# A fused attention and feed-forward layer on one core: fewer and earlier first loads, batch 1 normalised ahead, two moves in the last block

## The chip, the core and the metric

The kernel runs on one core of one Trainium2 chip. TensorE (PE) does the matmuls and the transposes, VectorE (DVE), ScalarE (ACT) and GpSimd (POOL) work beside it, and SyncE (SP) issues the DMAs. Each engine runs its own list of instructions strictly in order and meets the others by semaphores. The metric is the device time of one execution in microseconds; the number given for a kernel is the median of its runs.

## The reference

All data are float32. For x of shape (4, 512, 256) the layer is

```
x = x + layernorm(attn(layernorm(x)))
x = x + layernorm(ffn(layernorm(x)))
```

`attn` adds two things and multiplies the sum by Wo. The first is attention of 2 heads of 128 in windows of 128 tokens, each looking at its own and the previous 128 keys. The second is a memory that learns while it reads: for each of 4 batches and 4 heads of 64 it keeps three 64x64 states W0, W1, W2 and goes through the sequence in 4 chunks of 128 tokens:

```
q, k = l2norm(silu(x @ Wq)), l2norm(silu(x @ Wk));  v = silu(x @ Wv)
out  = (silu(q @ W0.T) * (q @ W2.T)) @ W1.T          # read with the chunk's states
dW*  = gradients of the same net for k, v and rates l0, l1, l2, plus momentum M* * mean(m)
dW*  = newtonschulz5(dW*)                            # 5 rounds: A = X X', B = bA + cAA, X = aX + BX
W*   = renorm(W* + dW*)                              # rows keep their first norm
```

The rates come from a softplus of x @ Wlr, m from a sigmoid of x @ Wm + bm; the read result is normalised, scaled by o_norm_g and by silu(x @ Ws + bs). `ffn` is a gelu layer 256 -> 1024 -> 256 with biases.

## The kernel before

The work is cut into 4 chunks of 128 tokens, each for all 4 batches. Every engine walks through the same written list `ORDER` of steps and does its own part of each step, if it has one. A step is written KIND.chunk.rest: `QK.0.1` is the product of chunk 0, batch 1, with the q and k weights. The list alone sets the order on PE, DVE, ACT and POOL. SP has its own code (lines 461 to 505), which doesn't follow the list. `bank_plan` goes through the list once and gives each step that writes PSUM the banks that come free first, so a step that leaves the list changes the banks of those behind it.

The steps that the change and the prediction speak of:

- `LN1.0.b` (line 1067): DVE takes mean and variance of the rows of batch b (line 1070, 1072), POOL makes the inverse root in two instructions, an addition of the epsilon (line 1424) and a power (line 1419). `LNX.0.b` (line 1087): DVE subtracts and multiplies. `XT.0.b` (line 536): PE transposes the rows, ACT copies them to `xnT` (line 816).
- `QK.0.b` (line 559) and `VV.0.b` (line 568): PE multiplies with the q/k weights (512 columns) and with the v weights and the 20 small ones (276 columns). Each float32 matmul instruction stands as two passes in the trace, so a QK step of two instructions is x4. ACT copies q and k to `raw` (line 816), DVE copies v to `v_rows` (line 1127) and adds the small biases (line 1135).
- `SI` (lines 873, 874): silu on ACT. `NQ`: square on ACT (line 886), sum on DVE (line 1141), root on POOL (line 1419). `NR`: reciprocal on DVE (line 1147), product on POOL (line 1419, `silu<-silu,rq`). `TR.0.0` to `TR.0.9` (line 591): transposes of q, k, v for the attention (0 to 3, from `raw`) and for the memory (4 to 9).
- `LN1.1`, `LNX.1`: the same normalisation for chunk 1, all batches at once; its rows come by `rows_in(1)`.
- `WI.0` (lines 1350 to 1361 on DVE, 1022 on ACT): DVE spreads the loaded states over the batches into `W`, ACT squares them. `WX.0.g` (line 723): PE transposes the states, ACT copies them to `WT02` and `W1T`.
- `SP.0`: rates on ACT and DVE. `S.0.b` (line 732): scores, masked on DVE (line 1298). `WN.0`: DVE sums the squares of the states (line 1365), which `FW.0.0` on ACT waits for (line 937). `DW.0` (line 662): the gradients, fed by `ELB` on DVE.
- `F2.3.b` (line 793): the last product of batch b; DVE adds the bias, takes statistics (lines 1378 to 1382), POOL makes the inverse root (lines 1424, 1419). `F2N.3.b` (lines 1387, 1056): DVE subtracts the mean, then multiplies by the inverse root and adds `x1`; SP stores (line 491).

Before the list PE runs 9 matmuls on a tile of ones (line 808), whose result nobody reads.

The signal that a DMA has landed is counted by a semaphore of its own per group: `ld_qkv`, `ld_small`, `ld_misc`, `ld_w`; `first_x[b]` for the rows of chunk 0.

Of the kernel before, what the change touches and what calls it, by code (L numbers as in the profile page):

```python
# [128 lines left out]
def steps(text):  # L129
# [17 lines left out]
    TR.1.3 NB.0.1.1 NB.0.1.2 NT.0.0 MS.1 NT.0.1 NT.0.2 NT.0.3 NX.0.1.0 NX.0.1.1 NX.0.1.2 TX.0.2.0 NQ.1.0 TX.0.2.1
    TX.0.2.2 NQ.1.1 SI.1.3 F1.0.0 NA.0.2.0 NA.0.2.1 NA.0.2.2 F1.0.1 F1.0.2 LN1.2 NB.0.2.0 NB.0.2.1 NB.0.2.2 NQ.1.2
    NR.1.0 NR.1.1 F1.0.3 F1.0.4 LNX.2 NX.0.2.0 NX.0.2.1 NX.0.2.2 NQ.1.3 TX.0.3.0 TX.0.3.1 TX.0.3.2 F1.0.5 NA.0.3.0
    NA.0.3.1 WR.0 NA.0.3.2 XT.2 F1.0.6 NB.0.3.0 NB.0.3.1 NB.0.3.2 MM.1 NR.1.2 NR.1.3 NX.0.3.0 NX.0.3.1 NX.0.3.2  # L150
    TX.0.4.0 KL.1.0 TX.0.4.1 TX.0.4.2 F1.0.7 NA.0.4.0 NA.0.4.1 NA.0.4.2 KL.1.1 TR.1.4 TR.1.5 F2.0.0 SP.1 NB.0.4.0
# [5 lines left out]
    WON.1.1 NA.1.0.0 NA.1.0.1 NA.1.0.2 SI.2.0 SI.2.1 CT.1.2 CT.1.3 L2.1.0 VV.2.2 VV.2.3 NB.1.0.0 NB.1.0.1 NB.1.0.2
    WO.1.2 WO.1.3 NQ.2.0 LN1.3 MS.2 L2N.1.0 NQ.2.1 NX.1.0.0 NX.1.0.1 NX.1.0.2 TX.1.1.0 WON.1.2 WON.1.3 TX.1.1.1
    TX.1.1.2 QK.2.3 NA.1.1.0 NA.1.1.1 NA.1.1.2 NB.1.1.0 NB.1.1.1 SI.2.2 NT.1.0 L2.1.1 L2.1.2 L2.1.3 L2N.1.1 TR.2.0
    TR.2.1 TR.2.2 TR.2.3 MM.2 NB.1.1.2 NX.1.1.0 NX.1.1.1 SM.2 NX.1.1.2 NR.2.0 L2N.1.2 NT.1.1 NT.1.2 L2N.1.3 TX.1.2.0  # L160
    TX.1.2.1 NR.2.1 LNX.3 TX.1.2.2 NT.1.3 NA.1.2.0 F2N.0.0 NA.1.2.1 SI.2.3 NQ.2.2 NQ.2.3 NA.1.2.2 NR.2.2 NR.2.3 KL.2.0
# [1417 lines left out]
```

## Time and profile before

| | |
|---|---|
| median of 3 runs | 382.04 us (381.73 to 382.21) |
| span of the profiled execution, first to last instruction | 380.1 us (380.141) |
| median less span | 1.9 us |
| PE busy | 371.0 us, 98% of the span |
| DVE, ACT, POOL busy | 257.6, 213.3, 193.9 us |
| bytes read from HBM, written | 7.73 MB, 2.10 MB |

The profiled execution has no time of its own beside its span. The span counts from the first to the last instruction; what lies around it is taken as the 1.9 us by which the median is above it. Times below are in microseconds from the start of the span. A busy PE isn't PE at its peak: its matmuls are pipelined and their ends modelled, so that the starts of two matmuls tell more than the length of one.

### The profile page before, as it was taken

To read this page: it belongs to the slowest core of one execution; us is meant where nothing else is said; L and a number is where in the kernel's file an instruction comes from. 1 tells how busy PE (TensorE), PEld (TensorE's weight loads), DVE (VectorE), ACT (ScalarE), POOL (GpSimd) and SP (SyncE) were. 2 spreads that over 40 slices of the span, in tenths; PEclk is the share of its full clock that TensorE was granted. 3 is DMA by queue.
4 is the path that set the end of the run, shared out by engine and by line. 5 is a ranking of instruction groups with operands and counts; after the bars stand their busy time and mean duration, and the time that the engine had idled before them with its cause. 6 is when DMAs were issued, how large, how long until landed. Compare 5 with 4: busy or idle time off the path is not lost.

```text
span 380.1 us, 15979 instructions
## 1 busy us (share of the span) xinstructions
PE 371.0 (98%) x6760; PEld 295.4 (78%) x6760; DVE 257.6 (68%) x682; ACT 213.3 (56%) x432; POOL 193.9 (51%) x290
## 2 busy tenths in 40 slices
PE   8999999999999999999999999999999999999994
PEld 5588688856788877878578888688887757988883
DVE  4678998674278699898546746987875492767124
ACT  1799855766512766649743346665358575614500
POOL 4399865356239457475963434364333340557212
PEclk9999999999999999999999999999999999999999
DMA  5562200001000000000000200000000110000101
GB/s 156 121 238 60 83 1 6 3 3 46 16 3 2 3 3 2 3 4 5 16 19 17 71 16 3 2 2 17 20 3 4 40 36 2 0 3 0 57 0 55
DMA packets 12677, 10.84 MB, mean 29 GB/s; under 512 B 4544, under 2 KB 12096, under 8 KB 12608
## 3 DMA queue, kind: packets, MB, share of 16 engines
q1 hardware_dynamic: 12608, 9.83, 8.9%
q8 instruction: 54, 0.88, 1.0%
q14 instruction: 15, 0.12, 0.1%
HBM read 7.73 MB, written 2.10 MB: 26 GB/s over the span
## 4 chain that ended last, share of the span: by engine, by line
PE 86%; DVE 4%; SPq 3%; issue 2%; POOL 2%; ACT 1%; DMA 1%; POOLq 0%; DVEq 0%; ACTq 0%
PE pair L782 15%; PE pair L793 15%; PE pair L713 6%; PE pair L701 6%; PE pair L691 6%; PE pair L559 6%; PE pair L682 5%; PE pair L591 4%; PE pair L763 3%; PE pair L732 3%; PE pair L568 3%; PE pair L748 3%; PE pair L662 2%; PE pair L739 2%; PE pair L629 1%
## 5 line engine op out<-in xcount | busy, mean ns | idle before, releaser
L782 PE MATMUL pair<-xn2T,p1T 128*128 128x512 f32 (+1 forms) x160 | 59.1, 512 | 0.0
L793 PE MATMUL pair<-p2T,h 128*128 128x256 f32 x256 | 57.0, 379 | 0.0
L793 PEld LDWEIGHTS pair<-p2T,h 128*128 128x128 f32 x256 | 48.0, 190 | 6.4 <-issue 0.2
L1424 POOL TENSOR_SCALAR var<-mv 128x1 f32<-128x1 f32 (+1 forms) x55 | 13.1, 239 | 67.1 <-DVE mv L1382 37.4
L1034 ACT ACTIVATE h<-pair,b 128x512 f32<-128x512 f32 (+1 forms) x40 | 23.9, 602 | 36.0 <-PE pair L782 35.9
L782 PEld LDWEIGHTS pair<-xn2T,p1T 128*128 128x128 f32 x160 | 28.7, 190 | 17.1 <-issue 14.8
L1419 POOL TENSOR_TENSOR nq<-ssq,half 128x8 f32<-128x8 f32 (+1 forms) x16 | 24.2, 1513 | 27.5 <-DVE ssq L1141 27.5
L1056 DVE SCALAR_TENSOR_TENSOR A<-pair,eye 128x512 f32<-128x512 f32 x45 | 28.7, 683 | 13.2 <-PE pair L691 13.1
L1419 POOL TENSOR_TENSOR rstd<-var,neg_half 128x1 f32<-128x1 f32 (+1 forms) x55 | 33.5, 609 | 4.6
L1056 DVE SCALAR_TENSOR_TENSOR B<-pair,eye 128x512 f32<-128x512 f32 x45 | 28.9, 684 | 10.2 <-PE pair L701 10.0
L559 PE MATMUL pair<-wqkv,xnT 128*128 128x512 f32 x64 | 31.5, 627 | 0.6 <-ACT xnT L816 0.6
L701 PEld LDWEIGHTS pair<-A 64*64 64x64 f32 x1440 | 23.7, 134 | 7.5 <-issue 4.6
L987 ACT ACTIVATE masked<-masked,nmax 128x256 f32<-128x256 f32 (+1 forms) x32 | 15.1, 474 | 25.5 <-DVE nmax L1298 25.5
L823 ACT ACT_TABLE_LOAD x22 | 28.2, 1283 | 1.1 <-PEq L1569 0.7
L691 PEld LDWEIGHTS pair<-XT 64*64 64x64 f32 x1440 | 23.3, 134 | 6.3 <-issue 5.7
L816 ACT ACTIVATE XT<-pair 128x512 f32<-128x512 f32 x45 | 24.6, 600 | 6.4 <-PE pair L682 6.4
L713 PEld LDWEIGHTS pair<-X,B 64*64 64x64 f32 x1440 | 23.6, 134 | 5.0 <-issue 2.7
L959 ACT ACTIVATE X<-pair 128x512 f32<-128x512 f32 x36 | 19.8, 598 | 13.2 <-PE pair L713 13.1
L701 PE MATMUL pair<-A 64*64 64x64 f32 x1440 | 26.5, 221 | 0.3 <-issue 0.3
L713 PE MATMUL pair<-X,B 64*64 64x64 f32 x1440 | 26.1, 221 | 0.1
L691 PE MATMUL pair<-XT 64*64 64x64 f32 x1440 | 25.8, 221 | 0.3 <-ACT XT L816 0.2
L682 PE MATMUL pair<-ident,X 128*128 128x128 f32 x180 | 24.1, 276 | 0.5 <-ACT X L959 0.3
(165 smaller groups left out, 775.4 us busy)
## 6 DMA issues: line engine op xcount, KB each, us to landing
x_in<-in_L_attn_x_dram SPq DMA_DIRECT2D x16, 128.0 KB, 2.5
x<-in_L_attn_x_dram SPq DMA_DIRECT2D x16, 128.0 KB, 2.1
out_dram<-rows_a SPq DMA_DIRECT2D x16, 128.0 KB, 1.7
p1T<-in_L_ffn_proj_dram SPq DMA_DIRECT2D x1, 1024.0 KB, 4.7
p2T<-in_L_ffn_proj_dram SPq DMA_DIRECT2D x1, 1024.0 KB, 7.4
wqkv<-in_L_attn_Wqkv_dram SPq DMA_DIRECT2D x1, 768.0 KB, 4.8
wo<-in_L_attn_Wo_dram SPq DMA_DIRECT2D x1, 256.0 KB, 7.7
X<-in_L_attn_w_dram SPq DMA_DIRECT2D x6, 32.0 KB, 2.2
```

What stands on the lines that cost most here:

```text
L559: mm_ = pe.matmul(ps, xnT[:, k, b * P:(b + 1) * P], wqkv[:, k, 0:512], start=(k == 0), stop=(k == KC - 1))
L682: mm_ = pe.transpose(ps[:, b * P:(b + 1) * P], X[:, g, 2 * b:2 * b + 2, :], ident[:, :])
L691: mm_ = pe.matmul(BANK[bank[0] + row][64 * col:64 * col + 64, n * HD:(n + 1) * HD], xt, xt, start=True, stop=True)
L701: mm_ = pe.matmul(BANK[bank[0] + row][64 * col:64 * col + 64, n * HD:(n + 1) * HD], a, a, start=True, stop=True)
L713: mm_ = pe.matmul(BANK[bank[0] + row][64 * col:64 * col + 64, n * HD:(n + 1) * HD], B[64 * row:64 * row + 64, g, 4 * (row ^ (slot & 1)) + ...
L782: mm_ = pe.matmul(ps[:, at], p1T[:, k, n * P:(n + 1) * P], xn2T[:, k, at], start=(k == 0), stop=(k == KC - 1))
L793: mm_ = pe.matmul(ps[:, 0:DIM], h[:, n, b * P:(b + 1) * P], p2T[:, n, :], start=(n == 0), stop=(n == HC - 1))
L816: return act.activation(dst, src, ACT.Copy)
L823: act.preload_act_table_set(name)
L1034: act.activation(h[:, n, at], BANK[bank[0]][:, at], ACT.Gelu, bias=b1[:, n:n + 1]).then_inc(S["h"].sem, 1)
L1056: return dve.scalar_tensor_tensor(out=out_, in0=in0, scalar=scalar, in1=in1, op0=op0, op1=op1)
L1419: return pool.tensor_tensor(out_, in0, in1, op)
```

## The change

It has four parts.

1. The loads at the start. The weights of q, k, v and the small ones stand in one array `Wall`, whose first 512 columns (q and k) are loaded before the rows of batches 1 to 3 and the other 276 behind them; seven loads of constants are one (`packed`, 356 columns per partition, the rows already repeated over the partitions). The three states come already spread over the batches and also transposed (`states`, 128 partitions x 3072), into `W`, `WT02` and `W1T`. So DVE's copies of `WI.0`, the steps `WX.0.*` and one memset are gone. The arrays are laid out outside the kernel (`laid_out`). SP now follows the list as well, with the steps `XI.c` (rows of chunk c for the normalisation) and `XA.c` (rows for the residual).
2. `LNX.0.1` stands before `LN1.0.3` and `CO.0`. Behind the transposes of batch 0 (`XT.0.0`) PE runs 3 matmuls of 64 columns on the tile of ones, whose result nobody reads.
3. At the end `F2N.3.2` stands before `F2.3.3`.
4. For the last block (chunk 3, batch 3) the epsilon is added on DVE, and POOL only takes the power.

```diff
-    LN1.0.0 XT.0.0 LNX.0.0 LN1.0.1 LN1.0.2 CO.0 LN1.0.3 LNX.0.1 QK.0.0 XT.0.1 LNX.0.2 LNX.0.3 VV.0.0 VV.0.1 SI.0.0
+    LN1.0.0 XT.0.0 LNX.0.0 LN1.0.1 LN1.0.2 LNX.0.1 LN1.0.3 CO.0 XA.0 QK.0.0 XT.0.1 LNX.0.2 LNX.0.3 VV.0.0 VV.0.1
...
-    F1.3.6.1 F1.3.7.1 F2.3.0 F2.3.1 F2N.3.0 F2.3.2 F2N.3.1 F2.3.3 F2N.3.2 F2N.3.3
+    F1.3.1.1 F1.3.2.1 F1.3.3.1 F1.3.4.1 F1.3.5.1 F1.3.6.1 F1.3.7.1 F2.3.0 F2.3.1 F2N.3.0 F2.3.2 F2N.3.1 F2N.3.2
+    F2.3.3 F2N.3.3
...
             sp.dma_start(x_in[:, 0, :], x[0, 0:CHUNK, :]).then_inc(first_x[0], 16)
-            sp.dma_start(wqkv[:, :, 0:3 * DIM], Wqkv.rearrange("(k p) n -> p k n", p=P)).then_inc(ld_qkv, 16)
+            sp.dma_start(wqkv[:, :, 0:512], Wall[:, 0:512].rearrange("(k p) n -> p k n", p=P)).then_inc(ld_qkv, 16)
             for b in range(1, BATCH):
                 sp.dma_start(x_in[:, b, :], x[b, 0:CHUNK, :]).then_inc(first_x[b], 16)
...
-            sp.wait_ge(ld_qkv, 16)
-            for n, w in enumerate((w1, w2, w0)):
...
-            rows_in(1)
+            sp.dma_start(wqkv[:, :, 512:], Wall[:, 512:].rearrange("(k p) n -> p k n", p=P)).then_inc(ld_v, 16)
+            sp.dma_start(packed_in[:, :], packed).then_inc(ld_misc, 16)
+            sp.dma_start(W[:, :, :, :], states[:, 0:1536].rearrange("p (g s d) -> p g s d", s=8, d=HD)).then_inc(ld_w, 16)
+            sp.dma_start(WT02[:, :, :, :, :], states[:, 1536:2560].rearrange("p (b j k d) -> p b j k d", j=2, k=2, d=HD)).then_inc(ld_wT, 16)
+            sp.dma_start(W1T[:, :, :, :], states[:, 2560:3072].rearrange("p (b j d) -> p b j d", j=2, d=HD)).then_inc(ld_wT, 16)
+            XI(1)
...
                     mm_.then_inc(S["first_xT"].sem, 1)
+                    if b == 0:
+                        for n in range(3):
+                            pe.matmul(BANK[7][:, 0:64], ones[:, :], ones[:, 0:64], start=True, stop=True)
                     return
...
                 dve.bn_aggr(mv4[:, b, :], st4[:, b, :]).then_inc(S["f2_mv"].sem, 1)
+                if ends(c, b):
+                    dve.wait_ge(*S["f2_mv"](c, b + 1))
+                    dve.tensor_scalar(var4[:, b:b + 1], mv4[:, b, 1:2], LN_EPS, None, ALU.add).then_inc(S["f2_var"].sem, 1)
...
             def F2(c, b):
+                if ends(c, b):
+                    wait_apart(pool, S["f2_var"](c, b + 1))
+                    tt(rstd4[:, b:b + 1], var4[:, b:b + 1], neg_half[:, 0:1], ALU.pow).then_inc(S["f2_rstd"].sem, 1)
+                    return
                 rsqrt(c, b + 1, mv4, var4, rstd4, "f2_mv", "f2_var", "f2_rstd", slice(b, b + 1))
```

How the lists of instructions change, at three places. First SP at the program's start, before and then changed (`Wlr`, `Wm`, `Ws`, `bm` and so on are the small inputs; `in_L_attn_w_dram` a state; `first_xn` rises when batch b is normalised):

```order
L462 DMA wqkv<-in_L_attn_Wqkv_dram 128x2x768
L464 DMA x_in<-in_L_attn_x_dram 128x256 x3
L465 DMA wqkv<-in_L_attn_Wlr_dram 128x2x12
L466 DMA wqkv<-in_L_attn_Wm_dram 128x2x4
L467 DMA wqkv<-in_L_attn_Ws_dram 128x2x4
L468 DMA small_bias<-in_L_attn_bm_dram 128x4
...
L479 DMA X<-in_L_attn_w_dram 64x2x64 [waits ld_qkv]
L479 DMA X<-in_L_attn_w_dram 64x2x64 x5
L459 DMA x_in<-in_L_attn_x_dram 128x256 [waits s_first_xn]
L459 DMA x_in<-in_L_attn_x_dram 128x256 x3
```

```order
L473 DMA wqkv<-in_Wall_dram 128x2x512
L475 DMA x_in<-in_L_attn_x_dram 128x256 x3
L476 DMA wqkv<-in_Wall_dram 128x2x276
L477 DMA packed_in<-in_packed_dram 128x356
L478 DMA W<-in_states_dram 128x1536
L479 DMA WT<-in_states_dram 128x1024
L480 DMA W1T<-in_states_dram 128x512
L464 DMA x_in<-in_L_attn_x_dram 128x256 [waits s_first_xn]
L464 DMA x_in<-in_L_attn_x_dram 128x256 x3
```

In front of chunk 1's rows (the last two rows of each) there stood 21 loads and stand 10, batch 0's rows ahead of those shown counted in. Second, PE in chunk 0 behind the transposes TR.0.4 to TR.0.7, before and then changed:

```order
L591 MATMUL pair<-ident,silu 128x128 x3
L723 MATMUL pair<-ident,W 128x128 [waits s_W,s_att_T]
L723 MATMUL pair<-ident,W 128x128 x3
...
L732 MATMUL pair<-akT,aqT 128x128 [waits s_att_T,s_xnT]
...
L568 MATMUL pair<-wqkv,xnT 128x276 [waits s_xnT,s_ttt_T,ld_small]
...
L591 MATMUL pair<-ident,silu 128x128 [waits s_qn,s_WT]
```

```order
L585 MATMUL pair<-ident,silu 128x128 x3
L726 MATMUL pair<-akT,aqT 128x128 [waits s_att_T]
...
L562 MATMUL pair<-wqkv,xnT 128x276 [waits s_xnT,ld_v]
...
L585 MATMUL pair<-ident,silu 128x128 [waits s_qn,s_ttt_T]
```

The 12 transposes of the states are gone from between TR.0.7 and the scores; TR.0.9 (the last row of each) waits for `qn` in both. Third, DVE at the program's end, before and then changed:

```order
L1387 TENSOR_SCALAR rows_a<-rows_a,mv 128x256 [waits s_f2_mv]
L1056 SCALAR_TENSOR_TENSOR rows_a<-rows_a,rstd,x 128x256 [waits s_f2_rstd,s_f2_n,consts]
L1378 TENSOR_TENSOR rows_a<-pair,b 128x256 [waits s_f2_ps]
L1380 BN_STATS st<-rows_a 128x6 [waits s_f2]
L1382 BN_AGGR mv<-st 128x2 [waits s_f2_st,consts]
L1387 TENSOR_SCALAR rows_a<-rows_a,mv 128x256 [waits s_f2_mv]
L1056 SCALAR_TENSOR_TENSOR rows_a<-rows_a,rstd,x 128x256 [waits s_f2_rstd,s_f2_n,consts]
L1387 TENSOR_SCALAR rows_a<-rows_a,mv 128x256 [waits s_f2_mv]
L1056 SCALAR_TENSOR_TENSOR rows_a<-rows_a,rstd,x 128x256 [waits s_f2_rstd,s_f2_n,consts]
```

```order
L1371 TENSOR_SCALAR rows_a<-rows_a,mv 128x256 [waits s_f2_mv]
L1051 SCALAR_TENSOR_TENSOR rows_a<-rows_a,rstd,x 128x256 [waits s_f2_rstd,s_f2_n,consts]
L1359 TENSOR_TENSOR rows_a<-pair,packed_in 128x256 [waits s_f2_ps]
L1361 BN_STATS st<-rows_a 128x6 [waits s_f2]
L1363 BN_AGGR mv<-st 128x2 [waits s_f2_st,consts]
L1366 TENSOR_SCALAR var<-mv 128x1 [waits s_f2_mv]
L1371 TENSOR_SCALAR rows_a<-rows_a,mv 128x256 [waits s_f2_mv]
L1051 SCALAR_TENSOR_TENSOR rows_a<-rows_a,rstd,x 128x256 [waits s_f2_rstd,s_f2_n,consts]
```

The pair L1387, L1056 of batch 2 stood behind the statistics of batch 3 and stands before them; the new row L1366 is the epsilon.

## Rows read from the trace of the kernel before

**Rows 1.** The page: busy time by engine, and the last chain by engine.
```profile
PE 371.0 (98%) x6760; PEld 295.4 (78%) x6760; DVE 257.6 (68%) x682; ACT 213.3 (56%) x432; POOL 193.9 (51%) x290
...
PE 86%; DVE 4%; SPq 3%; issue 2%; POOL 2%; ACT 1%; DMA 1%; POOLq 0%; DVEq 0%; ACTq 0%
```

**Rows 2.** Chain that ended last, 0 to 50 us: start, us, what.
```profile
12.10 0.59 SPq L459
...
14.10 2.25 DMA x_in<-in_L_attn_x_dram
...
16.38 1.42 DVE st L1077 x4
...
19.63 0.49 ACT raw L816
```

**Rows 3.** Timeline, 0 to 45 us: start, us, engine, line, operation, [idle before].
```profile
6.50 3.75 PE L559 MATMUL pair<-wqkv,xnT 128*128 128x512 f32 x4 [0.56 <-ACT xnT L816]
...
9.99 0.41 DVE L1087 TENSOR_SCALAR rows_b<-x_in,mv,rstd 128x256 f32<-128x256 f32 x1 [0.46 <-POOL rstd L1419]
10.05 0.61 PE L536 MATMUL pair<-ident,rows_b 128*128 128x128 f32 x2
...
14.72 0.60 ACT L816 ACTIVATE raw<-pair 128x512 f32<-128x512 f32 x1 [0.40 <-PE pair L559]
...
18.70 0.63 ACT L873 ACTIVATE silu<-raw 128x512 f32<-128x512 f32 x1 [0.45 <-DVE small L1135]
```

**Rows 4.** Groups by line and shape, PE, 6.4 to 10.3 us: busy, mean ns.
```profile
L559 PE MATMUL pair<-wqkv,xnT 128*128 128x512 f32 x4 | 3.8, 1094 | 0.6 <-ACT xnT L816 0.6
```

**Rows 5.** The same from 12.9 to 16.2 us.
```profile
L559 PE MATMUL pair<-wqkv,xnT 128*128 128x512 f32 x8 | 3.6, 592 | 0.0
```

**Rows 6.** Windows: busy of PE, PEld, DVE, ACT, POOL; granted clock, DMA share, GB/s.
```profile
2.00:6.00 4.00, 3.91 (x18) 3.24 (x16) 1.02 (x3) 0.02 (x1) 2.00 (x8) 1.00 0.94 295
18.00:22.00 4.00, 3.71 (x23) 2.72 (x22) 3.37 (x16) 3.21 (x7) 3.40 (x5) 1.00 0.97 367
```

**Rows 7.** Timeline, 20 to 46 us, the engines that meet there.
```profile
25.17 1.47 PE L723 MATMUL pair<-ident,W 128*128 128x128 f32 x12
...
27.62 2.04 POOL L1419 TENSOR_TENSOR silu<-silu,rq 128x512 f32<-128x512 f32 x2
...
28.09 0.63 DVE L1056 SCALAR_TENSOR_TENSOR lr<-small,lr_log 128x48 f32<-128x48 f32 x1 [0.20 <-ACT lr_log L851]
...
29.23 1.20 PE L591 MATMUL pair<-ident,silu 128*128 128x128 f32 x8
...
32.49 0.60 ACT L937 ACTIVATE B<-pair 128x512 f32<-128x512 f32 x1 [0.15 <-DVE row_ss L1365]
...
42.87 0.69 DVE L1191 TENSOR_TENSOR h<-h 128x512 f32<-128x512 f32 x1
```

**Rows 8.** Timeline, small DVE instructions of chunk 0.
```profile
7.64 0.07 DVE L1060 MEMSET small_bias<- 128x12 f32 x1
...
23.40 0.37 DVE L1115 TENSOR_SCALAR ms<-ms_t 128x16 f32<-128x16 f32 x1 [0.60 <-ACT ms_t L856]
```

**Rows 9.** Timeline, 366 to 380 us, POOL and DVE.
```profile
366.28 0.57 POOL L1419 TENSOR_TENSOR rstd<-var,neg_half 128x1 f32<-128x1 f32 x1
...
375.00 0.42 DVE L1378 TENSOR_TENSOR rows_a<-pair,b 128x256 f32<-128x256 f32 x1 [1.47 <-PE pair L793]
...
375.98 0.18 DVE L1382 BATCH_NORM_AGGREGATE mv<-st 128x2 f32<-128x6 f32 x1
...
376.33 0.22 POOL L1424 TENSOR_SCALAR var<-mv 128x1 f32<-128x1 f32 x1 [2.37 <-DVE mv L1382]
376.49 0.48 DVE L1056 SCALAR_TENSOR_TENSOR rows_a<-rows_a,rstd,x 128x256 f32<-128x256 f32 x1
376.63 0.78 POOL L1419 TENSOR_TENSOR rstd<-var,neg_half 128x1 f32<-128x1 f32 x1
...
377.54 0.48 DVE L1056 SCALAR_TENSOR_TENSOR rows_a<-rows_a,rstd,x 128x256 f32<-128x256 f32 x1 [0.29 <-POOL rstd L1419]
```

More of the change, by code:

```diff
@@ L147 @@
[L147 to L151, printed above, removed]
@@ L157 @@
[L157 to L161, printed above, removed]
@@ L182 @@
-    F2N.2.1 F2N.2.2 F2N.2.3 F1.3.6.0 NT.3.3 F1.3.7.0 L2N.3.3 F1.3.0.1 F1.3.1.1 F1.3.2.1 F1.3.3.1 F1.3.4.1 F1.3.5.1
-    F1.3.6.1 F1.3.7.1 F2.3.0 F2.3.1 F2N.3.0 F2.3.2 F2N.3.1 F2.3.3 F2N.3.2 F2N.3.3
+    LN1.0.0 XT.0.0 LNX.0.0 LN1.0.1 LN1.0.2 LNX.0.1 LN1.0.3 CO.0 XA.0 QK.0.0 XT.0.1 LNX.0.2 LNX.0.3 VV.0.0 VV.0.1
+    SI.0.0 NQ.0.0 XT.0.2 XT.0.3 QK.0.1 SI.0.1 WI.0 LN1.1 QK.0.2 VV.0.2 NQ.0.1 LNX.1 XI.2 SI.0.2 NR.0.0 QK.0.3
+    VV.0.3 NR.0.1 NQ.0.2 TR.0.0 SM.0 TR.0.1 SI.0.3 MS.0 NQ.0.3 TR.0.2 TR.0.3 XT.1 TR.0.4 TR.0.5 TR.0.6 TR.0.7
@@ L231, with layer_kernel @@
 PLAN = bank_plan(ORDER)
-def layer_kernel(nc, x, Wqkv, Wlr, Wm, bm, Ws, bs, Wo, w0, w1, w2, o_norm_g, qk_scale, qk_offset,
-                 proj1T, proj1_bias, proj2T, proj2_bias, out):
+def layer_kernel(nc, x, Wall, packed, states, Wo, proj1T, proj2T, out):
     with ExitStack() as ctx:
@@ L434, in mask_of, with ends @@
             return mask[:, seen(c):2 * P] if slot(c) else mask[:, P:3 * P]
+        def ends(c, b):
+            return c == CHUNKS - 1 and b == BATCH - 1
         def learns(c):
@@ L485, in _, with run @@
             sp.dma_start(wo[:, :, :], Wo.rearrange("(k p) n -> p k n", p=P)).then_inc(ld_wo, 16)
-            rows_again(0)
-            def stores(c):
-                for b in range(BATCH):
-                    sp.wait_ge(*S["outb"](c, b + 1))
-                    sp.dma_start(out[b, bass.ts(c, CHUNK), :], outb[:, b, :]).then_inc(S["stored"].sem, 16)
-            rows_again(1)
-            rows_in(2)
-            rows_in(3)
-            stores(0)
-            rows_again(2)
-            stores(1)
-            rows_again(3)
-            stores(2)
-            stores(3)
+            def run(order):
+                for kind, c, *arg in order:
+                    if kind in parts:
+                        parts[kind](c, *arg)
+            run(ORDER)
             sp.wait_ge(*S["stored"](CHUNKS, 0))
@@ L610, in DH @@
                 pe.wait_ge(*S["ttt_T"](c, 6 if c else 2))
[L611 removed]
+                pe.wait_ge(*(S["W"](c, 1) if c else (ld_w, 16)))
                 for b in range(BATCH):
@@ L1058, in CO @@
             def CO(c):
-                dve.memset(small_bias[:, 0:12], BASE_LR_INV)
                 dve.memset(ones_avg[:, :], 0.5 / CHUNK)
@@ L1571 @@
     for name in _INS:
-        a = np.ascontiguousarray(inputs[name].T if name in _TRANSPOSED else inputs[name])
+        a = np.ascontiguousarray(laid_out(name, inputs))
         arrays[f"in_{name}_dram"] = a
```

174 lines of the change are left out of this document (92 added, 82 removed).

## The prediction

> **What bounds the kernel now.** I read the page's shares first. PE is busy for 98% of the span and carries 86% of the chain that ended last [rows 1]; nothing else is worth a cut in the middle, unless PE waits there. The 14% that isn't PE lies in the chain's first 20 us and its last 5, so I read those two in the order of time.
>
> At the start the chain runs through SP: it issues load behind load, comes to chunk 1's rows only at 12.10, issues the fourth of them at 14.10, and this lands 2.25 later, at 16.35 [rows 2]. DVE, strictly in order, has taken up LN1.1 by then (16.38, 1.42 us) and with it stands in front of the copy of batch 2's v. So ACT, idle for 0.45, starts SI.0.2 at 18.70 [rows 3], copies the last q/k product by 20.12 (19.63 + 0.49) [rows 2], and only then can PE start TR.0.0 at 20.26. This is one limit of the stage. The other is PE itself: the four passes of QK.0.0 run from 6.50 to the next start at 10.05 [rows 3], 1094 ns each, and the same passes later take 592 [rows 4, 5]; eight of them last 3.6 us by their starts, so four would need 1.72 (my estimate, less than half of 3.6 for the end of the last) and took 3.55. The windows view gives a granted clock of 1.00 there too [rows 6], but passes at double length are the lower of the two levels, 1.2 GHz, and after QK.0.0 the engine is at 2.4. Ahead of QK.0.0 PE had been idle for 0.56, waiting for ACT's copy of batch 0's rows [rows 3].
>
> At the end, PE gives its last product at 375.00. Add, statistics, aggregate (to 376.16), POOL's epsilon from 376.33, POOL's power from 376.63 to 377.41, DVE's last product at 377.54: all in a row [rows 9], then the store.
>
> **The change part by part.** The three small matmuls (six passes of half the columns of a transpose) lie in the 0.56 us of idle ahead of QK.0.0. A full transpose pass takes 0.11 at the higher clock (1.31 us for the 12 of [rows 7], by their starts), 0.22 at the lower, half of it 0.11; six are 0.66, about the hole, and I count 0. At full length they would be 1.3 and QK.0.0 0.75 late. What they can bring is the clock: PE then has no such hole in front of QK.0.0. If the clock rises at once at 6.50, QK.0.0 is over 1.83 sooner (3.55 - 1.72); if it rises where it does now, 0. I take 1.55, near the upper end, because the hole is the only one of this size there and QK.0.0 behind it alone was slow; so QK.0.0 ends at 8.5 instead of 10.05.
>
> The Trainium skill (TensorE: Matmul & The Clock Gate, "What's actually happening") says that activity releases the clock and that the point where this happens isn't tied to the kernel's start. By it the gain would come in some runs and be there already, or not come, in others. The three runs of before lie within 0.48 us, less than the 1.55, which doesn't bear this out; it is a rival below.
>
> Does the rest follow? Batch 1's rows: LNX.0.1 now directly follows LN1.0.2. The q/k load is 0.26 MB shorter, so batch 1's rows land about 0.6 sooner than 6.4; POOL's root is ready near 7.5, and XT.0.1 is ready at 8.0, ahead of PE's 8.5. The v weights and constants must be there at 8.7 and 10.5: in front of them 1.5 MB; at the 295 GB/s of 2 to 6 us [rows 6] that is 2.0 + 5.1 = 7.1. Then XT.0.1 (0.22), VV.0.0 and VV.0.1 (0.93 each, the second after ACT's copies at 9.75), XT.0.2 and XT.0.3 (0.44), QK.0.1 (1.71): over at 12.85. ACT can copy it at 13.05 instead of 14.72 [rows 3], 1.65 sooner. From there ACT is back to back up to the end of the fourth copy at 20.12, but for the 0.45 of idle: 20.12 - 14.72 - 0.45 = 4.95. That gives 18.0, and TR.0.0 at 18.15 instead of 20.26: **2.05 to 2.1 us**.
>
> This needs chunk 1's rows in time. SI.0.2 started 2.35 behind their landing (18.70 - 16.35); it is wanted at 16.65, so they must land by 14.3. SP now waits for batch 3's normalised rows: 10.40 before (9.99 + 0.41 [rows 3]), 10.1 now. Four issues at the spacing of before (12.10 to 14.10) and 2.25 give 14.35; at the 0.47 of SP's short issues, 13.9. So it just fits, with a cost of 0 to 0.1. The bytes: the states grow from 0.19 to 1.57 MB, 3.09 MB lie in front of chunk 1's rows. At 295 GB/s they are through at 12.5, at 367 [rows 6] at 10.4; the rows' 0.52 MB then end by 14.3 in the worse case.
>
> DVE's six copies of the states (about 1.4 us) and ACT's three lie beside waiting; nothing on the path. WX.0 is 12 passes, 1.3 us by their starts (25.17 to 26.48) [rows 7], on PE, the busy engine, yet I count **0** for it: a little later PE comes to TR.0.9, the second half of the 1.20 us from 29.23, which waits for POOL's last normalised q and k at 29.66 (27.62 + 2.04) [rows 7]. PE arrives sooner and waits for POOL. POOL's row of roots and products is itself fed by LN1.1 and by ACT's squares, and moves up by the same 2.05. Nor does PE get the time back later: DVE's rate instruction waits for ACT at 28.09, ACT's FW.0.0 waits at 32.49 for DVE's row sums, and the product that DW.0 needs from DVE ends at 43.56 (42.87 + 0.69) [rows 7], in the middle of DW.0. All of these move with ACT's chain. If POOL and DVE had room after all, up to 1.3 more could come; if the shorter chain meets something that doesn't move, less than 2.05.
>
> SP's new places for the residual rows and chunk 2's rows have tens of microseconds to spare. The bank plan is worked out anew, and most steps of chunks 0 to 2 stand in other banks; some wait for another reader than before. PE's stalls there are short, so I count 0; what it may cost is the fourth rival.
>
> The end. F2N.3.2 used to sit between the statistics and the last product; now it runs in the 3.4 us in which PE works on F2.3.3. Its product (376.49, 0.48) was beside POOL's power, which took 0.78 there and 0.57 at 366.28, where DVE stood still [rows 9]. The power now meets only the subtraction: 0.57 to 0.78, I take 0.60, saving 0.17. The epsilon on DVE: the trace has no such instruction of one column. From below 0.07 (a memset), from above 0.37 (16 columns on DVE) [rows 8]; I take 0.18, as the aggregate of two columns [rows 9]. It starts 0.04 behind 376.16, ends at 376.38, POOL follows 0.16 later as it does now: 376.54 against 376.63, saving 0.09 (between +0.10 lost and 0.20 saved). Together **0.25**, between 0.1 lost and 0.4 saved.
>
> The Trainium skill (SBUF — State Buffer, "Who interferes with whom") says that a DVE instruction with two SBUF inputs, or in a 2-port mode, locks out a POOL instruction that reads SBUF. For the product the trace agrees, 0.78 against 0.57. By the same rule the subtraction, with one input, might hold the port first and delay the power to its own end near 376.7, which would take back some 0.15 of the 0.25.
>
> Sum against the execution's own time: 380.14 - 2.05 - 0.25 = 377.84 of span, and 1.90 around it (382.04 - 380.14) makes **379.7**.
>
> **The rivals.** First, the clock rises where it does now, since the hole wasn't the reason. For it: PE was busy from 1.04 on with little idle and still slow. Against: the one large hole lies exactly there. Then PE holds ACT at 14.72, and only the 0.45 wait of ACT goes, 0.42 of it: 382.04 - 0.42 - 0.25 = 381.4.
>
> Second, by the page's rule, the clock's rise is scattered over the runs, and the median stands between the two: about 380.6.
>
> Third, chunk 1's rows land at 15.2 to 15.8, because the states are slow to move: each 0.1 behind 14.3 costs 0.1. At 15.3 it is 380.7.
>
> Fourth, the start's gain is given back in chunk 0 or 1, at a wait of another bank or on POOL, and only what the end saves is left, with a little of the start: 381.5.
>
> Fifth, slower: the same transfer, much worse. SP's queue puts 1.57 MB of states in front of chunk 1's rows, and DVE is blocked by LN1.1 until they come. Equal to now they would be at a landing of 16.35 plus the 0.25 of the end, and slower by what can be measured at 17.4. For this 3.6 MB would have to move at under 235 GB/s from 2.0 on. The lower of the two rates in the rows is 295 [rows 6], and that with many small pieces in it. At 220 GB/s the landing is at 18.4 and the time 382.04 + 2.05 - 0.25 = 383.8.
>
> **How the numbers follow.** Forecast 0.50 (379.7; own range 379.1 to 380.4); clock unmoved 0.24; scattered 0.08; rows late 0.05; given back 0.07; slower 0.06. About 0.2%, 0.76 us, is what a measurement of this kernel tells from no change; the border to faster lies at 381.28. The unmoved clock's 381.4 lies on it, half to each side. Faster: 0.50 + 0.12 + 0.08 + 0.05 = 0.75. Same: 0.12 + 0.07 = 0.19. Slower: 0.06. The range, 379.0 to 381.8, leaves out the slower case, part of the given back and what lies beyond the bounds of the forecast below.
>
> **What would show it.** In the profile of the changed kernel: the passes of QK.0.0 near 600 to 700 ns on average and not 1094; batch 1's rows transposed near 8.5; chunk 1's first statistics near 14 and not 16.38; no idle on ACT ahead of SI.0.2; TR.0.0 near 18.2; PE idle for about half a us or more ahead of TR.0.9; POOL's last power near 0.6, and the last DVE product 2.4 us behind the last bias addition (now 2.54) or less. It would be wrong if QK.0.0 stays at 1094, if LN1.1 still begins behind 16, or if PE's lead of 2 us at TR.0.4 is smaller at 60 us.

## The result, and the profile after

The changed kernel took 379.49 us (median of 4 runs, 379.32 to 380.99) beside 382.12 (381.73 to 382.39) for the kernel before: a ratio of 0.9937, 95% interval 0.9918 to 0.9955. Forecast were 379.7 and a range of 379.0 to 381.8. The profiled execution has a span of 377.6, where the sum said 377.84, and 1.8 around it.

The page of the changed kernel, busy time by engine and the last chain by engine:

```profile
PE 369.0 (98%) x6754; PEld 294.4 (78%) x6754; DVE 256.9 (68%) x676; ACT 212.1 (56%) x429; POOL 193.9 (51%) x289
...
PE 88%; DVE 5%; POOL 2%; issue 2%; ACT 2%; POOLq 0%; DVEq 0%; ACTq 0%
```

SP's queue and the DMA, which stood in the chain before [rows 1], are gone from it; that chunk 1's rows still hold the start only the experiments will show. The timeline of the changed kernel's start (start, us, engine, line, operation, [idle before it <- who ended it]):

```profile
6.75 1.94 PE L553 MATMUL pair<-wqkv,xnT 128*128 128x512 f32 x4
8.52 0.38 PE L527 MATMUL pair<-ident,rows_b 128*128 128x128 f32 x2
9.81 1.75 SPq L464 DMA_DIRECT2D x_in<-in_L_attn_x_dram  x4
13.10 0.60 ACT L810 ACTIVATE raw<-pair 128x512 f32<-128x512 f32 x1 [0.54 <-PE pair L553]
14.32 1.41 DVE L1071 BATCH_NORM_STATS2 st<-x_in 128x6 f32<-128x256 f32 x4 [1.59 <-DMA x_in<-in_L_attn_x_dram]
16.36 0.23 POOL L1408 TENSOR_SCALAR var<-mv 128x4 f32<-128x4 f32 x1 [1.56 <-DVE mv L1075]
16.64 0.63 ACT L867 ACTIVATE silu<-raw 128x512 f32<-128x512 f32 x1
18.21 1.94 PE L585 MATMUL pair<-ident,raw 128*128 128x128 f32 x16
26.75 0.63 PE L585 MATMUL pair<-ident,silu 128*128 128x128 f32 x4 [0.34 <-POOL silu L1403]
27.75 0.63 PE L585 MATMUL pair<-ident,silu 128*128 128x128 f32 x4 [0.37 <-POOL silu L1403]
28.31 1.10 PE L623 MATMUL pair<-tttT,WT 64*64 64x128 f32 x32
```

QK.0.0 starts 0.25 later than in [rows 3], since the six small passes take until 6.9, but is over at 8.52 and not at 10.05. Chunk 1's rows are there at 14.32 and not at 16.38 [rows 2]; DVE had waited 1.59 for them. TR.0.0 is at 18.21 and not at 20.26. The two lines at 26.75 and 27.75 show PE idle for POOL, in the stretch ahead of which WX.0 used to lie [rows 7]. FW.0.0, the last line, is at 28.31. In the kernel before, POOL's epsilon for chunk 1 (16.36 above) and FW.0.0 stood here:

```profile
18.43 0.23 POOL L1424 TENSOR_SCALAR var<-mv 128x4 f32<-128x4 f32 x1 [1.82 <-DVE mv L1081]
...
30.36 1.10 PE L629 MATMUL pair<-tttT,WT 64*64 64x128 f32 x32
```

The group of QK.0.0's passes from 6.7 to 8.6 us (busy, mean ns), against 1094 ns in [rows 4], and the two windows that answer to [rows 6]:

```profile
L553 PE MATMUL pair<-wqkv,xnT 128*128 128x512 f32 x4 | 1.9, 606 | 0.0
```

```profile
2.00:6.00 4.00, 3.94 (x20) 3.68 (x19) 1.45 (x4) 0.00 (x0) 2.01 (x8) 1.00 0.99 313
18.00:22.00 4.00, 3.68 (x32) 3.29 (x31) 3.21 (x13) 3.66 (x9) 3.91 (x5) 1.00 1.05 364
```

The rates are about the ones of before; the 1.4 MB that came on top of them filled time in which the DMA engines had been half idle (a busy share of 0.37 to 0.56 from 6 to 12 us before, 0.89 to 0.96 now). The end of the changed kernel, against [rows 9]:

```profile
372.79 0.42 DVE L1359 TENSOR_TENSOR rows_a<-pair,packed_in 128x256 f32<-128x256 f32 x1 [0.42 <-PE pair L787]
...
373.78 0.18 DVE L1363 BATCH_NORM_AGGREGATE mv<-st 128x2 f32<-128x6 f32 x1
374.00 0.15 DVE L1366 TENSOR_SCALAR var<-mv 128x1 f32<-128x1 f32 x1
374.07 0.34 DVE L1371 TENSOR_SCALAR rows_a<-rows_a,mv 128x256 f32<-128x256 f32 x1
374.30 0.55 POOL L1403 TENSOR_TENSOR rstd<-var,neg_half 128x1 f32<-128x1 f32 x1 [2.55 <-DVE var L1366]
374.98 0.49 DVE L1051 SCALAR_TENSOR_TENSOR rows_a<-rows_a,rstd,x 128x256 f32<-128x256 f32 x1 [0.57 <-POOL rstd L1403]
```

From the last bias addition to the last product it is 374.98 - 372.79 = 2.19, before 2.54. So of the 2.54 us that the span lost (380.14 to 377.6), 0.35 is the end, 2.05 the start up to FW.0.0 (30.36 to 28.31), and 0.14 lies between. The 0.35 and the 2.05 are firm, the 0.14 is not. The end takes 2.54 in both profiles with the old end and 2.18 or 2.19 in all eleven that have the changed end whole. But from FW.0.0 to the last bias addition the same code takes 344.25 to 344.64 in three profiles of the changed kernel, and 344.01 and 344.64 in the two with the old code.

### The profile page after: what moved, and what is told of

It reads as the page before. It is cut to its first block, busy times and chain, and to the rows that moved or that the text cites. A ratio compares the mean times of both kernels' runs of the same rounds, so it can differ in the third digit from the quotient of the medians.

```text
span 377.6 us, 15942 instructions
## 1 busy us (share of the span) xinstructions
PE 369.0 (98%) x6754; PEld 294.4 (78%) x6754; DVE 256.9 (68%) x676; ACT 212.1 (56%) x429; POOL 193.9 (51%) x289
## 4 chain that ended last, share of the span: by engine, by line
PE 88%; DVE 5%; POOL 2%; issue 2%; ACT 2%; POOLq 0%; DVEq 0%; ACTq 0%
PE pair L776 15%; PE pair L787 15%; PE pair L553 7%; PE pair L695 6%; PE pair L685 6%; PE pair L707 6%; PE pair L676 5%; PE pair L757 3%; PE pair L562 3%; PE pair L585 3%; PE pair L726 3%; PE pair L742 3%; PE pair L656 2%; PE pair L733 2%; PE pair L623 1%
## 5 line engine op out<-in xcount | busy, mean ns | idle before, releaser
L1029 ACT ACTIVATE h<-pair,packed_in 128x512 f32<-128x512 f32 (+1 forms) x40 | 23.9, 602 | 36.1 <-PE pair L776 36.1
L553 PE MATMUL pair<-wqkv,xnT 128*128 128x512 f32 x64 | 29.7, 597 | 0.0
L676 PE MATMUL pair<-ident,X 128*128 128x128 f32 x180 | 24.1, 276 | 0.5 <-ACT X L954 0.3
```

What stands on the lines that cost most here:

```text
L553: mm_ = pe.matmul(ps, xnT[:, k, b * P:(b + 1) * P], wqkv[:, k, 0:512], start=(k == 0), stop=(k == KC - 1))
L676: mm_ = pe.transpose(ps[:, b * P:(b + 1) * P], X[:, g, 2 * b:2 * b + 2, :], ident[:, :])
L1029: act.activation(h[:, n, at], BANK[bank[0]][:, at], ACT.Gelu, bias=b1[:, n:n + 1]).then_inc(S["h"].sem, 1)
```

## The experiments

In each group the kernel before ran on the same chip; its median was 381.59 in the first, 382.12 in the second and 381.97 in the third, so ratios are compared and not times. The first group has after_again, no_small, before_small and rows_first_wi, the second rows_late, wx_back, rows_each_wi and end_eps_old, the third after_third, cold, rows_each and rows_each_wi2; the second has no run of the changed kernel itself.

**The changed kernel again**, first and third group, unchanged.

> The changed kernel once more, beside the others. What is asked is how far its single times lie apart. Theory 1 (the three small matmuls fill the hole ahead of QK.0.0 and the clock rises there in every execution): all times within 0.6 of 379.5. Rival (the clock's rise is scattered between 6 and 10 us, whatever the matmuls do): a share of the times stands 1 to 1.5 above the rest, as 380.99 did beside 379.3 to 379.6.

> The changed kernel again, as the measure of the others on this chip: 378.9 to 379.5, with one time in ten near 381.

Measured 378.88 (378.61 to 379.29, 5 runs; ratio 0.9929, 0.9917 to 0.9940) and 379.45 (379.28 to 379.92, 5 runs; ratio 0.9933, 0.9919 to 0.9948). No run is near 381 among these ten; 378.61 lies more than 0.6 below 379.5, but so does its whole group, the kernel before with it. Over all kernels here that have the small matmuls and early rows there were three: 380.99 in the first measurement, 381.21 in wx_back, 380.62 in rows_each_wi2, out of 41. If these are late clocks, which no profile shows, a late clock is rare with the small matmuls, not excluded.

**Without the three small matmuls.**

```diff
-                    if b == 0:
-                        for n in range(3):
-                            pe.matmul(BANK[7][:, 0:64], ones[:, :], ones[:, 0:64], start=True, stop=True)
```

> The changed kernel without the three small matmuls behind batch 0's transposes. Theory 1: QK.0.0 starts 0.25 sooner (6.50), but its passes take 1.09 us as before and end near 10.05; ACT's copy of QK.0.1 comes at 14.7 and TR.0.0 near 19.7; 381.0 (380.7 to 381.3). Rival, the matmuls don't set the clock's rise: QK.0.0 is as fast as now and even 0.25 sooner, 379.2 to 379.6.

Measured 379.84 (378.91 to 380.89, 6 runs; ratio 0.9957, 0.9941 to 0.9972). The six are 378.91, 379.08, 379.74, 379.95, 380.28 and 380.89: they are spread from the changed kernel's time to 2 us above it. The profiled execution is a quick one: QK.0.0 runs from 6.31 to 8.10 although the hole of 0.56 is there. So neither theory holds as it was written. The median is 0.3% worse without the matmuls than with them in the same group; the two intervals, 0.9917 to 0.9940 and 0.9941 to 0.9972, just don't touch, but that of the first measurement (up to 0.9955) and that of after_third (up to 0.9948) do overlap with it. An effect is likely, its size open.

What the profile can't tell is what the hole does to the clock, because the clock was up before the hole began. The warm-up's 18 passes take 4.21 us where all are at the lower level; here they take less, and the pass behind them is short too:

```profile
1.04 3.98 PE L799 MATMUL pair<-ones 128*128 128x128 f32 x18 [1.04 <-DVE ones L1046]
5.33 0.41 PE L527 MATMUL pair<-ident,rows_b 128*128 128x128 f32 x2 [0.31 <-DVE rows_b L1078]
```

In the same way the passes of the eleven profiles that have the small matmuls say where the clock rose. In four it was inside the warm-up (before_small, after_again, wx_back, rows_each), in two between the warm-up and the small matmuls (after_third, rows_late), and there the small matmuls can have had no part in it. In five it was within the six small passes or at their end (0.83 to 1.26 us for the six, against 0.78 at the higher level): the changed kernel, end_eps_old, rows_first_wi, rows_each_wi, rows_each_wi2. Whether in these five the rise would have come so early without the small matmuls is not shown; no execution with the hole and the clock still low ahead of it was profiled but the kernel before and cold, and in both the clock rose only behind QK.0.0.

**The small matmuls alone, in the kernel before.** The same lines, added.

> The kernel before with the three small matmuls alone. Theory 1 with two limits in a row: QK.0.0 ends near 8.5 and ACT's copy of QK.0.1 comes near 13.1, but chunk 1's rows still land at 16.35, LN1.1 stands on DVE ahead of the copy of batch 2's v, and TR.0.0 stays at 20.26 or comes at most 0.2 sooner: 381.8 to 382.1. Rival, the clock alone carries the gain and the rows are no limit: TR.0.0 1.5 sooner, 380.5.

Measured 381.69 (381.09 to 381.98, 11 runs; ratio 0.9999, 0.9990 to 1.0007). The gain is nothing, with an interval narrow enough to say so. From its timeline:

```profile
6.27 1.95 PE L562 MATMUL pair<-wqkv,xnT 128*128 128x512 f32 x4
...
16.09 1.40 DVE L1080 BATCH_NORM_STATS2 st<-x_in 128x6 f32<-128x256 f32 x4 [1.09 <-DMA x_in<-in_L_attn_x_dram]
...
19.97 1.94 PE L594 MATMUL pair<-ident,raw 128*128 128x128 f32 x16 [0.98 <-ACT raw L819]
...
30.07 1.10 PE L632 MATMUL pair<-tttT,WT 64*64 64x128 f32 x32
```

The clock is high and QK.0.0 over at 8.0, 2 us sooner than in the profile of before. PE then stands idle for 0.98 ahead of TR.0.0, which comes 0.29 sooner, just as much as the rows landed sooner (16.09 against 16.38).

**Chunk 1's rows made late.** p2T's load of 1 MB is issued ahead of them.

```diff
+            sp.dma_start(p2T[:, :, :], proj2T.rearrange("(n p) e -> p n e", p=P)).then_inc(ld_p2, 16)
             XI(1)
```

> The changed kernel with the 1 MB load of the second feed-forward weights (p2T) issued ahead of chunk 1's rows. It prices the rows' landing. Theory (at 14.3 the rows sit at the edge of the path): 1.05 MB more at about 0.36 MB per us land the rows near 16, LN1.1 stands on DVE ahead of batch 2's v, SI.0.2 comes near 18.3 and TR.0.0 near 19.8: 1.5 to 1.7 slower than the changed kernel, 380.4 where that takes 378.9. Rival, PE and POOL have room behind LN1.1: at most 0.5 slower.

Measured 382.15 (381.06 to 382.91, 12 runs; ratio 0.9995, 0.9983 to 1.0008): the whole gain is gone.

```profile
17.23 1.41 DVE L1071 BATCH_NORM_STATS2 st<-x_in 128x6 f32<-128x256 f32 x4 [4.74 <-DMA x_in<-in_L_attn_x_dram]
...
21.11 1.94 PE L585 MATMUL pair<-ident,raw 128*128 128x128 f32 x16 [3.02 <-ACT raw L810]
...
31.21 1.10 PE L623 MATMUL pair<-tttT,WT 64*64 64x128 f32 x32
```

The landing moved by 2.91 against the profile of the changed kernel, more than the 1.7 expected: at the 0.36 MB per us that I had assumed, 1.05 MB take 2.9, so the added bytes cost their whole time. FW.0.0 moved by 2.90. The price per us is one to one there, as the theory has it. The profiled execution (382.91) is among the slowest of the twelve and loses another 0.6 behind FW.0.0, where the edit has no part that I know of.

**WX.0 put back.** Twelve transposes of the states in S.0.0's bank, ahead of its product; nothing reads them.

```diff
+                if b == 0 and c == 0:
+                    pe.wait_ge(ld_w, 16)
+                    for g in range(3):
+                        for m in range(4):
+                            pe.transpose(ps[:, m * P:(m + 1) * P], W[:, g, 2 * m:2 * m + 2, :], ident[:, :])
```

> The changed kernel with 12 transposes of the states put back on PE, right ahead of S.0.0, where WX.0 stood; their result is not read. Theory (POOL's last normalised q and k for TR.0.9 hides them): PE's two waits of 0.34 and 0.37 ahead of TR.0.8 and TR.0.9 go, and TR.0.9 is late by what exceeds them: 1.3 - 0.9 = 0.4 to 0.5 late at TR.0.9 at most, 379.0 to 379.3. Rival, PE is the bound there: the full 1.3, 380.2.

Measured 379.42 (378.98 to 381.21, 6 runs; ratio 0.9928, 0.9907 to 0.9949), like the changed kernel. Its timeline, and under it the one of after_again, whose rows landed at the same time:

```profile
22.85 1.47 PE L727 MATMUL pair<-ident,W 128*128 128x128 f32 x12
24.16 1.06 PE L731 MATMUL pair<-akT,aqT 128*128 128x128 f32 x8
25.06 2.03 PE L562 MATMUL pair<-wqkv,xnT 128*128 128x276 f32 x8
26.92 1.20 PE L585 MATMUL pair<-ident,silu 128*128 128x128 f32 x8
28.05 1.10 PE L623 MATMUL pair<-tttT,WT 64*64 64x128 f32 x32
```

```profile
26.49 0.63 PE L585 MATMUL pair<-ident,silu 128*128 128x128 f32 x4 [0.34 <-POOL silu L1403]
27.49 0.63 PE L585 MATMUL pair<-ident,silu 128*128 128x128 f32 x4 [0.37 <-POOL silu L1403]
28.05 1.10 PE L623 MATMUL pair<-tttT,WT 64*64 64x128 f32 x32
```

FW.0.0 starts at 28.05 in both. PE's work of 1.3 us is worth nothing there; the expectation had granted it 0.4 to 0.5.

**The last epsilon back on POOL** (`ends` returns False; one profile). The product of the third block stays where the change put it.

> The changed kernel with the last epsilon back on POOL; the third block's product stays ahead of the fourth block's sum. The measure is the time from the start of the last bias addition to the start of the last product on DVE: 2.54 in the kernel before, 2.19 in the changed one. Theory (the product beside the power cost 0.2, the epsilon's place the rest): 2.30 to 2.37. Rival (the power is slow beside any DVE work, so moving the product gave nothing): 2.50 to 2.54.

```profile
372.94 0.43 DVE L1359 TENSOR_TENSOR rows_a<-pair,packed_in 128x256 f32<-128x256 f32 x1 [0.43 <-PE pair L787]
...
374.27 0.31 POOL L1408 TENSOR_SCALAR var<-mv 128x1 f32<-128x1 f32 x1 [2.38 <-DVE mv L1363]
374.66 0.57 POOL L1403 TENSOR_TENSOR rstd<-var,neg_half 128x1 f32<-128x1 f32 x1
375.36 0.48 DVE L1051 SCALAR_TENSOR_TENSOR rows_a<-rows_a,rstd,x 128x256 f32<-128x256 f32 x1 [0.86 <-POOL rstd L1403]
```

375.36 - 372.94 = 2.42, between the two theories. The power is short again (0.57), but POOL's epsilon takes 0.31 instead of 0.22; it now lies wholly beside a subtraction, of which it had met the last 0.07 before. So the product's move gave 0.12 and the epsilon's place 0.23. The order of before with the epsilon on DVE wasn't run.

**The clock held low on purpose.** No small matmuls and 3 warm-up matmuls instead of 9.

> The changed kernel without the three small matmuls and with 3 instead of 9 warm-up matmuls (the warm-up's result is never read), so that PE stands idle from about 2.3 to 5.3 and the clock must still be low at QK.0.0. It prices a late rise of the clock in the changed kernel. Theory: the four passes of QK.0.0 take about 1.05 each, QK.0.0 ends 1.7 to 1.9 later than at 8.1, ACT's copy of QK.0.1 and TR.0.0 come 1.5 to 2.5 later: 380.6 to 381.4 where the changed kernel takes 378.9 to 379.4, and the single times are as high as the two odd ones (380.99 and 381.21). Rival, POOL's row behind LN1.1 hides part of it: under 380.2.

Measured 383.61 (381.98 to 385.53, 12 runs; ratio 1.0042, 1.0024 to 1.0060), far above both. The profiled execution has a span of 383.7:

```profile
6.49 3.75 PE L550 MATMUL pair<-wqkv,xnT 128*128 128x512 f32 x4 [0.56 <-ACT xnT L807]
...
20.49 1.94 PE L582 MATMUL pair<-ident,raw 128*128 128x128 f32 x16
...
260.54 0.27 PE L682 MATMUL pair<-XT 64*64 64x64 f32 x1 [1.27 <-issue]
...
297.69 0.82 PE L704 MATMUL pair<-X,B 64*64 64x64 f32 x39 [1.35 <-issue]
```

The start is as expected: QK.0.0 at the lower level to 10.04, VV.0.0 partly too, TR.0.0 at 20.49, 2.28 later than in the changed kernel, with PE waiting for nobody. That is worth 2.1 at FW.0.0 (30.43). From there to the last bias addition it takes 348.52, about 4 more than the 344.0 to 344.6 of twelve others. Two waits of PE in the middle, for nothing the profile shows, are 2.6 of these; the other 1.3 or so are spread over several places. Their link to the edit is not settled. The profiled execution, 385.53, is one of the two slowest of the twelve, so cold prices the late clock at FW.0.0 and not by its median.

**Rows first, squares later.** The three loads of the states behind XI(1), and WI.0 (ACT's squares) behind SP.0.

```diff
-    SI.0.1 WI.0 LN1.1
+    SI.0.1 LN1.1
...
-    KL.0.3 SP.0 S.0.0
+    KL.0.3 SP.0 WI.0 S.0.0
...
+            XI(1)
             sp.dma_start(W[:, :, :, :], states[:, 0:1536].rearrange("p (g s d) -> p g s d", s=8, d=HD)).then_inc(ld_w, 16)
...
-            XI(1)
```

> The changed kernel with chunk 1's rows issued ahead of the three loads of the states, and ACT's squares of the states (WI.0) moved from ahead of SI.0.2 to the gap behind SP.0. Theory: chunk 1's rows, now landing at 14.3 in front of an idle DVE, are the next limit together with WI.0's 0.92 us on ACT. The rows land at 12.2 to 13.2, LN1.1 starts there, SI.0.2 at 15.7, POOL's row of roots 1 us sooner, TR.0.9 at 26.7 to 27.2 instead of 27.75: 378.3 to 379.0. Rival, POOL's own work between 16.36 and 27.6 is the limit whatever feeds it, or the squares behind SP.0 make the row sums late: 379.3 to 379.9.

Measured 379.11 (378.77 to 379.27, 5 runs; ratio 0.9933, 0.9922 to 0.9945). That is between the two ranges, and beside the changed kernel of its group (0.9929) no gain, as the rival has it. The rows landed at 13.88, little sooner, though the states were no longer in front of them: SP came to them only at 10.17, behind batch 3's normalisation, which frees the buffer. The states' bytes aren't free, though. From SP's first issue to the landing it took 3.71 here, 4.10 to 4.51 in the three profiles of the changed kernel.

**Rows batch by batch**, first with the squares moved (twice), then alone.

```diff
-                sp.wait_ge(*(S["xn"](c - 1, 1) if c > 1 else S["first_xn"](0, BATCH)))
+                if c > 1:
+                    sp.wait_ge(*S["xn"](c - 1, 1))
                 for b in range(BATCH):
+                    if c == 1:
+                        sp.wait_ge(*S["first_xn"](0, b + 1))
```

> The changed kernel with each batch's rows of chunk 1 issued as soon as that batch's rows of chunk 0 are normalised (instead of all four behind the last), and ACT's squares of the states moved behind SP.0. Theory (SP's wait for the fourth batch, not the bytes in front, sets the landing): only one issue is left behind 9.8, the rows land at 12.4 to 12.8 instead of 14.3, LN1.1 starts there, batch 1's sum of squares comes 0.6 sooner, POOL's row of roots with it, and TR.0.9 is at 26.7 to 27.0 where the changed kernel has 27.5 to 27.75: 0.5 to 0.8 faster, 378.1 to 378.4 beside 378.9. Rival, PE, back to back from 6.3 to 17.9, and POOL's own work leave nothing: 378.7 to 379.1.

> Rows of chunk 1 issued batch by batch and ACT's squares behind SP.0, again, now beside the changed kernel on one chip. Theory: TR.0.9 comes 0.5 to 0.6 sooner at the same start of QK.0.0: 0.3 to 0.6 faster than the changed kernel here. Rival: the two are the same within 0.2.

> The changed kernel with each batch's rows of chunk 1 issued as soon as that batch's rows of chunk 0 are normalised, the squares left where they are. Theory: the rows land at 13.5 instead of 14.1 to 14.5, LN1.1 starts there, but batch 1's sum of squares still waits for ACT, whose squares (0.92) stand ahead of the product it reads: 0 to 0.3 faster than the changed kernel. Rival: the landing alone carries what rows_each_wi has: 0.5 faster.

Measured with the squares moved: 379.11 (378.97 to 379.31, 5 runs; ratio 0.9915, 0.9898 to 0.9932) and 379.14 (378.67 to 380.62, 6 runs; ratio 0.9929, 0.9910 to 0.9948). The first theory (378.1 to 378.4) is missed; the second time is 0.31 below the changed kernel's, which isn't clear of the scatter. The rows land at 13.57 and 13.33, not at 12.4 to 12.8, and TR.0.9 is at 27.51 in the first and not at 26.7 to 27.0. FW.0.0 is at 28.07 and 27.82, some 0.5 later than the landing alone would have it: POOL waits 0.35 for DVE, and PE is back to back up to TR.0.0 in both, from a QK.0.0 that started late (6.91, 6.66). So what moving the squares is worth stays open. Alone, beside the changed kernel in the same group: 378.80 (378.67 to 378.88, 4 runs; ratio 0.9913, 0.9897 to 0.9929) against 379.45. All four lie below all five of the changed kernel (379.28 to 379.92), and the ratio to it is 0.998 (0.997 to 0.999, worked out from the single times). The rival was right here, the landing alone carries it, though its 0.65 us is from so few runs that its size is not firm. The last of the four loads is issued at 10.09 and no longer at 11.13 to 11.43, and lands 3.77 later. In rows_first_wi, without the states ahead, it was issued at 11.50 and landed 2.38 later. SP's wait and the states' bytes are thus again two limits close together: without the bytes the rows land at 13.88, without the wait at 13.33 to 13.86.

```profile
13.86 1.40 DVE L1074 BATCH_NORM_STATS2 st<-x_in 128x6 f32<-128x256 f32 x4 [1.03 <-DMA x_in<-in_L_attn_x_dram]
...
27.84 1.10 PE L626 MATMUL pair<-tttT,WT 64*64 64x128 f32 x32
```

This is the version to keep.

## What the traces say together

LN1.1 starts when chunk 1's rows have landed, but in cold, where they are there at 13.95 and DVE is late. Read from the timeline of each profiled execution:

| kernel | QK.0.0 starts | LN1.1 starts | TR.0.0 | FW.0.0 | FW.0.0 - LN1.1 |
|---|---|---|---|---|---|
| before | 6.50 (slow) | 16.38 | 20.26 | 30.36 | 13.98 |
| before_small | 6.27 | 16.09 | 19.97 | 30.07 | 13.98 |
| changed | 6.75 | 14.32 | 18.21 | 28.31 | 13.99 |
| after_again | 6.30 | 14.07 | 17.95 | 28.05 | 13.98 |
| after_third | 6.27 | 14.60 | 18.48 | 28.58 | 13.98 |
| no_small | 6.31 | 14.27 | 18.15 | 28.24 | 13.97 |
| rows_late | 6.46 | 17.23 | 21.11 | 31.21 | 13.98 |
| rows_each | 6.29 | 13.86 | 17.91 | 27.84 | 13.98 |
| rows_each_wi | 6.91 | 13.57 | 18.36 | 28.07 | 14.50 |
| rows_each_wi2 | 6.66 | 13.33 | 18.12 | 27.82 | 14.49 |
| cold | 6.49 (slow) | 15.07 | 20.49 | 30.43 | 15.36 |

wx_back, end_eps_old and rows_first_wi give 13.97 or 13.98 too. In 11 of the 14 executions, with landings from 13.86 to 17.23, PE's FW.0.0 comes 13.97 to 13.99 behind the landing, with a fast or slow QK.0.0, with or without WX.0. What lies between is DVE's statistics and then POOL: from its epsilon (16.36 in the changed kernel, 18.43 before) it works in a row to TR.0.9's last input. The second limit is PE: where it is back to back from QK.0.0 on, TR.0.0 comes 11.45 to 11.6 behind QK.0.0's start. With a slow QK.0.0 I add 1.8, the difference of the two QK.0.0 in this kernel and the one before (10.05 - 6.50 against 8.52 - 6.75); in cold, where VV.0.0 is slow too, it is 14.00 in all. In the kernel before that would have been 6.50 + 11.45 + 1.8 = 19.75, half a us ahead of the 20.26 that the rows allowed: the slow clock was there, and hidden. In the changed kernel's profile the two limits meet: 14.32 + 3.88 = 18.20 and 6.75 + 11.45 = 18.20.

## Why the prediction was right, and where not

**The start, 2.05 to 2.1: right in size (2.05), wrong in how it was charged.** I put 1.55 down to the clock and 0.45 to the rows, as a sum. It is the later of two limits. The rows' landing moved by 2.06, FW.0.0 by 2.05. The small matmuls alone are worth 0 (before_small). They can be worth something only once the rows are early: PE's limit with a slow QK.0.0 would then be 6.50 + 11.45 + 1.8 = 19.75 instead of 18.2, 1.5 late. The edit that carries the gain is the rows': with the small matmuls but late rows it is gone (rows_late, before_small), with early rows but no small matmuls more than half of it is there (0.9957 against 0.9929). So it is in part luck that the sum of two terms hit the time: 1.55 + 0.45 is close to the 2.06 by which the landing alone moved. Every sign that the prediction named was seen (606 ns, 8.52, 14.32, 18.21, PE idle for 0.34 and 0.37 ahead of TR.0.8 and TR.0.9, 0.55, 2.19, a lead that holds at 60 us), and none of them could tell a sum from a maximum. The single times of 380.6 to 381.2 stand that far above the others; that they are executions with a late clock is argued from the size, since none of them was profiled.

**"If it rises where it does now": partly the second rival.** The clock's rise is scattered: in six of the eleven profiles with the small matmuls, and in the one of no_small, it came before the place of the hole. Without the matmuls the times were spread over 2 us; with them three of 41 times stand out. The Trainium skill (TensorE: Matmul & The Clock Gate, "What's actually happening") has it that activity releases the clock at a point not tied to the kernel's start; the runs agree (the same 18 passes took 3.66 to 4.21). I had held the three times of before, 0.48 apart, against it. They couldn't bear on it, because there the rows hid the clock.

**The first rival, 381.4 with the clock unmoved,** has the right size for such an execution (19.75 against 20.26, and the end: 0.5 + 0.35), but with the small matmuls it would be one in some fourteen, not the median.

**The small matmuls at 0:** 0.25 late in the first profile, where the clock rose only near their end and QK.0.0 started at 6.75; in after_again and after_third the clock was up before they began, and QK.0.0 started at 6.30 and 6.27. That is inside the bounds, but the price of a pass was wrong:

```profile
5.75 1.16 PE L531 MATMUL pair<-ones 128*128 128x64 f32 x6
5.58 0.78 PE L531 MATMUL pair<-ones 128*128 128x64 f32 x6
```

The upper line is from the changed kernel, the lower from after_again. By their starts the passes of 64 columns are 0.21 apart at the lower level and 0.11 at the higher, as far as passes of 128 columns are. I had taken half of that. Six of them at the lower level would be 1.3 us, which the prediction names as the bad case; only the rise within them kept it to 0.25.

**The rows "just fit" at 14.3:** they landed at 14.07 to 14.60, and each tenth counts, as said. The edge was real but the reason was POOL's row behind LN1.1 and not only ACT's; and what sets the landing is SP's wait for the fourth batch and the states' bytes, two limits close together, as rows_first_wi and rows_each show. The slower rival (the same transfer, much worse) has its mechanism confirmed by rows_late, whose median is that of the kernel before.

**WX.0 at 0 and the bank plan at 0:** the first is shown (28.05 in both). Of the second only the sum can be seen: the lead is 2.05 at FW.0.0, 2.04 at 60 us and 2.21 at the last bias addition (375.00 to 372.79). The one at 60 us is from the same four transposes of X, at 61.80 (L682) and at 59.76 (L676). Nothing was given back that stands out of the 0.4 to 0.6 by which this stretch differs between profiles of one code.

**The end, 0.25:** 0.35, the same sum with its terms off. The product's move gave 0.12 (I said 0.17); what is missing fits the longer epsilon of POOL beside the subtraction. The epsilon on DVE gave 0.23 (I said 0.09): it takes 0.15, and POOL's slow one (0.31) is gone with its hand-over. The port rule that I had weighed (the Trainium skill, SBUF — State Buffer, "Who interferes with whom") speaks of a lock for the 2-port modes and of no contention for an instruction with one SBUF input outside them; had the subtraction run in a 2-port mode, it could have delayed the power. It didn't: the power started at 374.30 under the running subtraction (374.07 to 374.41) and took 0.55. For this subtraction, with one SBUF input, the traces show a slower POOL neighbour once (0.31 for 0.22), and no lock.

## What to carry to other kernels

Two waits that end near each other are a maximum and not a sum: ask of each edit alone what the other limit leaves of it, as the small matmuls show, worth 0 in one kernel and 0.96 by the medians of one group in the next (379.84 to 378.88, a size that isn't firm). When a load is late, look both at what its issue waits for (here a buffer freed by the fourth of four batches) and at the bytes in front. And where a chain behind one landing runs in a row on one engine, the distance from landing to its end is a constant that a handful of traces will show.
